# Turning keys and queries without TensorE in a two-layer attention kernel

## The reference

```
h = layernorm(x[b]);  q = h @ Wq + bq          # 16 heads of 128
k = ctx[b] @ Wk + bk; v = ctx[b] @ Wv + bv     # 4 heads of 128, each for 4 query heads
q = q * rsqrt(mean(q*q) + 1e-6) * qn_w         # over each head's 128
k = k * rsqrt(mean(k*k) + 1e-6) * kn_w
p = softmax(q @ k.T / sqrt(128) + mask)        # 128 x 128 per head
x[b] = x[b] + concat(p @ v) @ Wo
```

## Time and profile before

| | us |
|---|---|
| median of 3 runs (lowest, highest) | 835.23 (834.18, 835.74) |
| the profiled execution | 833.15 |
| its span, first to last instruction | 831.4 |
| mean granted TensorE clock | 0.983 of full |

### The profile page before, as it was taken

One profiled execution on the slowest core, in us unless ns is written; L12 is line 12 of the kernel. 1 busy time (PEld: TensorE's weight loads), 2 busy tenths in 40 slices (PEclk: granted clock), 3 DMA queues, 4 the chain that ended last, 5 costly groups with the idle time before them and its releaser, 6 DMA issues. The chain is left out here.

```text
span 831.4 us, 14178 instructions
## 1 busy us (share of the span) xinstructions
PE 787.2 (95%) x3968; PEld 654.6 (79%) x3968; DVE 566.4 (68%) x1049; ACT 470.7 (57%) x1618; POOL 548.3 (66%) x611
## 2 busy tenths in 40 slices
PE   6999996999999999999999999999987799989997
PEld 4888874888888888888888888888865577877886
DVE  4545455687787787787787787778777688754122
ACT  4555455575675675675665665665654256554440
POOL 2333355677777777776776876876867297756980
PEclk9999997999999999999999999999999899999999
DMA  7666663222322332332332332332254655213620
GB/s 231 200 212 205 200 218 97 60 82 68 103 83 68 102 90 64 101 91 67 95 95 63 96 94 63 98 91 63 76 158 155 231 186 182 103 54 125 204 99 25
DMA packets 85001, 97.66 MB, mean 117 GB/s; under 512 B 8112, under 2 KB 48176, under 8 KB 84976
## 3 DMA queue, kind: packets, MB, share of 16 engines
q1 hardware_dynamic: 84400, 95.52, 37.6%
q0 software_dynamic: 576, 1.84, 0.6%
HBM read 63.77 MB, written 17.30 MB: 98 GB/s over the span
## 5 line engine op out<-in xcount | busy, mean ns | idle before, releaser
L900 POOL TENSOR_TENSOR wp_lo<-raw,wp_hi 128x512 fp32r<-128x512 f32 x88 | 113.9, 1336 | 34.8 <-ACT wp_hi L970 34.8
L1080 ACT ACTIVATE p_row<-s_row,neg_max 128x128 f32<-128x128 f32 x256 | 100.0, 395 | 63.8 <-DVE neg_max L1374 63.7
L824 POOL TENSOR_TENSOR p_row<-p_row,p_inv 128x512 f32<-128x512 f32 x64 | 66.8, 1044 | 98.1 <-DVE p_inv L1389 98.1
L1794 PE MATMUL b_y<-wo_hi,oT_hi 128*128 128x512 f32 x256 | 107.5, 420 | 3.4 <-DVE oT_lo L1278 3.4
L1796 PE MATMUL b_y<-wo_hi,oT_lo 128*128 128x512 f32 x256 | 101.8, 398 | 0.0
L1795 PE MATMUL b_y<-wo_lo,oT_hi 128*128 128x512 f32 x256 | 101.8, 398 | 0.0
L1794 PE MATMUL b_q<-wq_hi,xT_hi 128*128 128x512 f32 x248 | 97.8, 394 | 0.0
L1796 PE MATMUL b_q<-wq_hi,xT_lo 128*128 128x512 f32 x248 | 97.4, 393 | 0.0
L1795 PE MATMUL b_q<-wq_lo,xT_hi 128*128 128x512 f32 x248 | 97.3, 392 | 0.0
L970 ACT ACTIVATE oT_hi<-b_o 128x512 fp32r<-128x512 f32 x64 | 38.4, 599 | 102.2 <-PE b_o L1796 100.3
L856 POOL TENSOR_TENSOR pT_lo<-raw,pT_hi 128x512 fp32r<-128x512 f32 x62 | 81.0, 1307 | 0.9 <-ACT pT_hi L970 0.9
(11 more groups left out here) (369 smaller groups left out, 2206.3 us busy)
## 6 DMA issues: line engine op xcount, KB each, us to landing
raw<-raw SPq DMA_DIRECT2D x248, 64.0 KB, 2.1
cx<-in_ctx_dram SPq DMA_DIRECT2D x16, 256.0 KB, 2.7
raw<-in_L_xattn_Wq_dram SPq DMA_DIRECT2D x16, 256.0 KB, 2.7
raw<-in_L_xattn_Wo_dram SPq DMA_DIRECT2D x16, 256.0 KB, 3.2
v_store<-v_out SPq DMA_DIRECT2D x16, 256.0 KB, 3.3
k_store<-k_out SPq DMA_DIRECT2D x16, 256.0 KB, 2.0
xr<-in_x_dram SPq DMA_DIRECT2D x16, 256.0 KB, 3.1
v_raw<-v_store SPq DMA_DIRECT2D x16, 256.0 KB, 3.0
```

The source lines that it names most:

```text
L824: pool.tensor_tensor(p_row[:], p_row[:], per_head(p_inv, S), ALU.mult).then_inc(p_normed, 1)
L900: last = pool.tensor_tensor(wp_lo[n % NSLOT][:, c, :], raw[RAW_OF[n]][:, c, :], wp_hi[n % NSLOT][:, c, :].bitcast(fp32), ALU.subtract)
L1080: e = act.activation(place, row, ACT.Exp, bias=neg_max[:, h:h + 1], accum_out=p_sum[:, h:h + 1])
L1794: pe.matmul(dst, left[0], right[0], start=start, stop=False)
```

## The change

Queries of batches 1 to 15 are turned as the probabilities are: VectorE transposes 32x32 blocks of the normalised rows (`q_turn`), four transfers of 64 KB set them in place (`load_q`), ScalarE makes the high part from SBUF (`loaded_q_high`), GpSimd the low part (`q_low`). The four quads of batch 0 are still turned by TensorE. Keys are turned in the same way on their way to DRAM: the block transpose is in `k_turn` (VectorE), four stores of 64 KB with rows of 512 bytes replace the one. Both norm weights, with the factor sqrt(128), are one row `k_gain`, which GpSimd multiplies into the normalised keys; neither ScalarE nor VectorE applies a weight any more.

GpSimd's normalisation of the probabilities goes to ScalarE, as four scaled copies. The query projection is one quad further ahead (t+2 for t+1), and GpSimd normalises q_row in place. x is loaded and normalised two batches ahead, in place; x(b+1) is turned in quad 1. Residual statistics, output norm, router scores and ranks come later by some quads, and `rank` reads the bank b_qT, which is free now. The loop covers batches 2 to 13; 0, 1, 14 and 15 are written apart. In the key stage SyncE stores v before it loads the next weights.

In the loop's quad t the orders are now: VectorE o_low(t-3), q_turn(t+1), q_bias(t+2), p_invert(t-1), what comes once a batch, p_turn(t-1), s_mask, s_sum and s_max(t); ScalarE o_high(t-3), v_high in quad 2, q_high(t), exps(t-1), p_high(t-2), x_high in quad 1, p_norm(t-1), squares(t+2), k_high in quad 3; GpSimd q_norm(t+1), q_low(t), one of k_low, base_rows and v_low in quads 0 to 2, p_low(t-2), out_stat in quad 3.

```diff
@@ SyncE
             def store_k(b):
-                sp.wait_ge(k_weighted, b + 1)
-                sp.dma_start(k_store[bass.ds(b * P, P), :], k_out[:]).then_inc(k_stored, 16)
+                sp.wait_ge(k_turned, b + 1)
+                for i in range(4):
+                    rows_ = k_store[b * P:(b + 1) * P, i * P:(i + 1) * P]
+                    sp.dma_start(rows_.rearrange("(j d) x -> d j x", j=4),
+                                 k_tr[32 * i:32 * i + 32].rearrange("d j g s -> d j (g s)")
+                                 ).then_inc(k_stored, 16)
...
+            def load_q(t, par):
+                sp.wait_ge(q_turned, t + 1)
+                for i in range(4):
+                    sp.dma_start(qT_in[par][:, i].rearrange("p h s -> p (h s)"),
+                                 q_tr[32 * i:32 * i + 32].rearrange("d j h s -> d j (h s)")
+                                 ).then_inc(qT_loaded, 16)
...
+                    if (i == NQUAD - 1 or not first) and (i < NQUAD - 1 or not last):
+                        load_q(t + 1, (i + 1) % 2)
+                    if i == 1 and has_old:
+                        store_base(b - 2)
                     if not (first and i == 0) and not (last and i == NQUAD - 1):
                         load_p(t - 1, (i - 1) % 2)
@@ GpSimd
-                pool.tensor_tensor(k_row[:], k_row[:], per_head(k_rs, HD), ALU.mult).then_inc(k_normed, 1)
+                wait(pool, k_turned, b)
+                pool.tensor_tensor(k_nrm, k_row[:], per_head(k_rs, HD), ALU.mult).then_inc(k_normed, 1)
+                pool.wait_ge(k_normed, b + 1)
+                pool.tensor_tensor(k_nrm, k_nrm, k_gain[:].unsqueeze(1).to_broadcast([P, NKV, HD]),
+                                   ALU.mult).then_inc(k_weighted, 1)
...
+            def q_low(t, par):
+                pool.wait_ge(qT_hi_done, t + 1)
+                pool.tensor_tensor(by_head(qT_lo), qT_in[par].rearrange("p i h s -> p h i s"),
+                                   by_head(qT_hi).bitcast(fp32), ALU.subtract).then_inc(qT_lo_done, 1)
@@ ScalarE
+            def loaded_q_high(t, par):
+                act.wait_ge(qT_loaded, 64 * (t - NQUAD + 1))
+                wait(act, scored, t)
+                copy(by_head(qT_hi), qT_in[par].rearrange("p i h s -> p h i s")).then_inc(qT_hi_done, 1)
...
+            def p_norm(t):
+                act.wait_ge(p_inverted, t + 1)
+                for h in range(QUAD):
+                    last = act.activation(p_row[:, h, :], p_row[:, h, :], ACT.Copy, scale=p_inv[:, h:h + 1])
+                last.then_inc(p_normed, 1)
@@ VectorE
+            def k_turn(b):
+                dve.wait_ge(k_weighted, b + 1)
+                wait(dve, k_stored, 64 * b)
+                dve.transpose(k_tr[:], k_nrm.rearrange("p g (j d) -> p j g d", j=4)).then_inc(k_turned, 1)
...
+            def q_turn(t):
+                dve.wait_ge(q_normed, t + 1)
+                if isinstance(t, int) and t == NQUAD:
+                    dve.wait_ge(q_turned, t)
+                else:
+                    dve.wait_ge(qT_loaded, 64 * (t - NQUAD))
+                dve.transpose(q_tr, q_row[:].rearrange("p h (j d) -> p j h d", j=4)).then_inc(q_turned, 1)
@@ TensorE
-            def turn_k(b, bank=b_kT):
-                pe.wait_ge(k_normed, b + 1)
-                wait(pe, k_weighted, b)
-                turn(bank, k_row[:].rearrange("p h d -> p (h d)")).then_inc(k_turned, 1)
...
-                        project_q(t + 1, b if i < NQUAD - 1 else b + 1, (i + 1) % NQUAD)
-                    turn_q(t)
+                    if first:
+                        turn_q(t)
...
+                    elif not (last and i >= 2):
+                        project_q(t + 2, b if i < 2 else b + 1, (i + 2) % NQUAD, banks=2 if first else 1)
-                    if i == 2 and not last:
+                    if i == 1 and not last:
                         turn_x(b + 1)
```

More of the change, by code:

```diff
@@ L243, in xattn_then_routed_ffn @@
             tied = sb_in(st, "tied", [P, 1])
+        qT_in = [row.rearrange("p (i h s) -> p i h s", i=4, h=QUAD) for row in (raw[1][:, 3, :], q_in1[:])]
         wo_place.close()
@@ L551, in keys_over, with ages @@
             eng.wait_ge(w_hi, 2 * NB)
+        def ages(kind):
+            first, last = kind == "first", kind == "last"
+            return first, last, kind not in ("first", "second"), kind not in ("late", "last")
         def layer1_over(eng):
@@ L703, in last_loads @@
                 sp.wait_ge(pT_lo_done, DMA_TURNED)
+                sp.wait_ge(qT_lo_done, STEPS)
                 sp.dma_start(raw[1][:], PIECES[1]).then_inc(raw_loaded[1], 16)
[L706 to L709, removed]
+            attend(0, "first")
+            attend(1, "second")
+            with sp.Fori(2, NB - 2) as b:
+                attend(b)
+            attend(NB - 2, "late")
+            attend(NB - 1, "last")
             def load_piece(n):
@@ L1014, in kv_batch @@
                 sq.then_inc(k_squared, 1)
-                if not first:
-                    weigh_k(b - 1)
                 if last:
@@ L1093, in attend @@
                         o_high(t - 3)
-                    if i == 2:
+                    if i == 2 and not first:
                         v_high(b)
-                    if (first and i < NQUAD - 1) or (last and i == NQUAD - 1):
+                    if first:
                         q_high(t)
+                    else:
+                        loaded_q_high(t, i % 2)
                     if first and i < NQUAD - 1:
@@ L1938, in _, with attend @@
             pe.wait_ge(v_biased, NB)
-            def attend(b, first, last):
+            def attend(b, kind="loop"):
+                first, last, has_old, has_far = ages(kind)
                 for i in range(NQUAD):
@@ L1958, in attend @@
                         add_y(t - 3, b if i == NQUAD - 1 else b - 1, (i + 1) % NQUAD)
-                    if i == NQUAD - 1 and not first and not last:
-                        spread_scores(b - 1, b + 2)
                     score_quad(t, b, i)
@@ L1963, in attend @@
                         mix(t - 2, b if i >= 2 else b - 1, (i + 2) % NQUAD)
-            attend(0, True, False)
-            with pe.Fori(1, NB - 1) as b:
-                attend(b, False, False)
-            attend(NB - 1, False, True)
+            attend(0, "first")
+            attend(1, "second")
+            with pe.Fori(2, NB - 2) as b:
+                attend(b)
+            attend(NB - 2, "late")
+            attend(NB - 1, "last")
             def turn_h(i):
```

313 lines of the change are left out of this document (184 added, 129 removed).

## The result

The changed kernel took 822.98 us (median of three runs, 822.67 to 823.17) against 835.23: ratio 0.986, 95% interval 0.984 to 0.988. It gains 12.2 us; 32.3 were forecast, and 823 lies just above the range. The profiled execution has a span of 821.1 us, 10.3 less than before. A second measurement, on the chip of three later experiments, gave 823.97 and a ratio of 0.9855.

A forecast was written before the change was run, and what follows sets the result against it. TensorE's own instruction count was taken to bound both stages. Query turns -27.0, key turns -6.9 and seams +1.6 sum to -32.3 us, from 835.2 to 803; range 797 to 822, the forecast's own 797 to 810.

The forecast's parts named there:

- The main claim: Key stage and loop: TensorE's instruction count sets the time; removed turns gain 6.9 us of keys and 27.0 of queries.
- the prediction's own test: Whole kernel: the forecast is wrong at its root if TensorE is dense and the time is above 810 us.
- The step that failed: Loop, VectorE: q_low goes, a block transpose of 0.702 us comes, so 6.2 us per quad stay, against TensorE's 7.30.
- Ring 1: Loop, scores to next output product: VectorE needs 3.0 us from mask to o_low, TensorE gives 3.4; slack 0.4 us.
- rival C: Loop: VectorE becomes the bound through a longer transpose or late o_high; quads of 7.5, 815 us; chance 0.10.
- Ring 3: Loop, probabilities: normalise, turn, transfer, high part take 6.6 us, 6.9 on average with x_high and a store, against 7.30.
- T: Loop, transfer of p within its ring: three issue slots of 0.63 and a landing of 2.1, together 4.0 us.
- rivals A and B: Loop, p's ring limits: A by landings of 2.8, 821 us, chance 0.15; B by transfers of 5.2, 851 us, chance 0.07.
- The seams: Head and end of the attention loop: gain of 1.0 us, loss of 2.6; net +1.6, bounds -4 to +5.

The follow-up runs named there:

- e13: Changed kernel with router's dot product in the second quad, x's load ahead of p's loads, third x's load issued earlier in the first batch: 805.83 us, ratio 0.9659.
- e4: Changed kernel with the router's dot product over 8 of the 512 columns, output not the reference's: 817.35 us, ratio 0.9789.
- e7: Changed kernel with the router's dot product moved from the first quad to the second and the ranking to the third: 813.36 us, ratio 0.9724.
- e11: Changed kernel with x's load issued ahead of p's loads and ScalarE normalising only the first of p's four heads, output not the reference's: 809.78 us, ratio 0.9695.
- e8: Changed kernel with the load of x issued ahead of p's loads and of x1's store in the second quad: 821.74 us, ratio 0.9826.
- e10: Changed kernel with ScalarE normalising only the first of p's four heads, x's load left late, output not the reference's: 823.25 us, ratio 0.987.
- e3: Changed kernel with GpSimd's normalisation of the fourth query ahead of the values' first low part in the first batch: 826.16 us, ratio 0.9895.
- e12: Changed kernel with the third x's load issued ahead of the router's weights and a 1 MB weight piece in the first batch: 821.57 us, ratio 0.9855.

## Why the prediction was wrong

**The main claim was right.** The instructions that leave TensorE are worth what was counted: 0.43 us for a turn of the keys, and 29.2 us for a batch with four query turns less. The second batch shows it in the changed kernel, and e13's loop (29.27) for all of them; e13 took 805.8 us, beside 834.6 for the kernel before on its chip, where 803 was forecast. So the forecast nearly holds for a kernel with three orders turned round, not for this one. By the prediction's own test it is not wrong at its root: that needed a dense TensorE above 810 us, and TensorE was not dense.

**The step that failed** is "VectorE ... Nothing is added; 80.47 of 100 at 7.75 is 6.2 us per quad". The diff moves the layernorm and the dot product of the routing from the fourth quad to the first, right ahead of p's turn, moves x's normalisation from the second to the fourth, and puts the queries' low part on GpSimd. VectorE's three operations then fall beside GpSimd's and take 4.04 us a batch instead of 1.77. VectorE's sum became 86.98 of 100 at 7.61, 6.6 us a quad instead of 6.2, and still under 7.30; it could not show what this costs, which is that p's turn is issued 1.6 us late. The kernel before's own trace had the price once, behind the loop, where the dot product ran beside GpSimd and took 1.41 us for 0.69, and the copy of the scores behind it 1.18 for 0.23:

```profile
614.01 1.41 DVE L1412 CUSTOM_DVE_ANT_0 dot_junk<-h_row,wr_row 128x512 bf16<-128x512 f32 x1
```

```profile
613.61 1.27 POOL L824 TENSOR_TENSOR p_row<-p_row,p_inv 128x512 f32<-128x512 f32 x1 [2.50 <-DVE p_inv L1389]
614.84 1.73 POOL L856 TENSOR_TENSOR pT_lo<-raw,pT_hi 128x512 fp32r<-128x512 f32 x1
```

The prediction had quoted the Trainium skill (SBUF — State Buffer, "Who interferes with whom") for the key stage, and not for the loop. In the key stage it came too, at no cost to TensorE: VectorE's splitting of wo rose from a mean of 0.68 to 1.43 us (10 to 110 us), in time in which VectorE had idled. The same section of the Trainium skill also names `tensor_scalar` in its two-port mode as one that takes the shared pair, and says that the later of the two "fully blocks". By 0.537 against 1.144 and 1.218 us, and by the 8 columns that take 1.15, these traces agree. So does the one scaling of x in the loop that VectorE began 0.08 us ahead of GpSimd (at 172.91): it took 0.53 us, and GpSimd's instruction 1.62 for about 1.30.

**Ring 1 left out what is queued in it.** "From the mixing's start, which is the scores' end, VectorE masks" took VectorE as free. In the third quad the statistics, p's turn, the moments and the residual stand ahead of the mask, and each waits or is waited for; the slack of 0.4 was used up by the 1.0 that the mask starts late. This was rival C's place, but not its reason.

**Ring 3 was sized well and joined to nothing.** From p's turn to the end of the next normalisation are 319.56 - 312.81 = 6.75 us, against 6.6 forecast, or 7.2 with the store that stands ahead of p's loads in this quad; T was 4.2 against 4.0, and landings stayed at 2.1. So rivals A and B fail by their own mechanism, and that A's time, 821, is nearly the one measured is chance. A ring with 0.4 us of slack cannot take in 1.6 us of delay before the third quad; that is how a cost in the first quad is paid two quads on, as e4, e7 and e11 show.

**A load that the sum does not have.** The diff normalises x in place, so the next x can only be loaded behind the turn of the last, and SyncE issues it behind p's four transfers. The prediction costed SyncE's time, 5.9 of 7.30, and not its order. In the loop that was 16.8 us of VectorE's waiting, worth some 2.4 us by itself (e8) and, if left, the whole of the ring's gain (e10 against e11).

**The seams.** The head was to gain 1.0 and lost 3.0: the trace shows VectorE's wait of 3.07 us for x, and its wait of 6.7 us ahead of the fourth query's bias, behind GpSimd's wait for v's high part. Neither move in the head (e3, e12) brought the 4 us back, so the cause stays open but for the load's part of up to 2 us. The end was forecast at two waits of 2.3 us; it has one of 2.13 for o_low and one of 4.06 ahead of the turn of the scores, whose making moved there:

```profile
597.32 0.50 PE L1908 MATMUL b_y<-wo_hi,oT_hi 128*128 128x512 f32 x1 [2.13 <-DVE oT_lo L1347]
606.53 0.30 PE L2029 MATMUL b_xT<-ident,score_wide 128*128 128x128 f32 x1 [4.06 <-issue]
```

VectorE ends the copy of the scores that this turn reads at 606.43; it took 1.17 us beside GpSimd instead of the 0.23 of the loop. Together the two waits are 1.6 us more than forecast, of the 2.5 that this stage is short; this was not tried apart, and neither was the 0.9 lost in the second layer.

## What to carry to other kernels

When a bound engine is relieved, check not the sum but the queue of each other engine: list what stands ahead of the instruction that closes a ring, with every moved operation and every load behind a moved issue in it. When an operation moves on VectorE, look up which GpSimd instruction it will run beside; its duration from the old place holds only for the old neighbour. And when an edit that should help does nothing, cross it with the next wait in the same queue before the theory is dropped: here one edit was worth 0 alone and 11 us beside the other. The reverse happens too: another did nothing alone and cost 0.4 us a batch in company.

## What the runs showed of the hardware

A VectorE dot product of 8 columns took as long as it took GpSimd to end the instruction that had begun before it (334.95 and 334.93 us): 1.15 us, against 0.17 where VectorE began first. The same happened to a one-input scale and shift of 128x512: 0.54 us with GpSimd elsewhere, 1.00 to 1.28 where GpSimd had begun first (26 times in the loop). VectorE's block transposes, reductions and passes that read PSUM kept their 0.65 to 0.71 us in the same windows. A 256 KB load issued 0.46 us behind a 1 MB one ended the wait of its reader 8 us after its issue; elsewhere its landing had a median of 2.8 us.
